# Opening reordered in a two-block LoRA kernel: one index table, the first weight split between tile pieces, GpSimd's subtractions behind a wait

## The reference

```python
# block 0: dense product and a mixture of 8 low-rank experts (rank 16), two chosen per token
base = einsum('btd,od->bto', x, W)
logits = einsum('btd,ed->bte', x, Wr) + 5.0 * one_hot(language_ids)
topw, topi = top_k(logits, 2)
gates = sum(one_hot(topi) * softmax(topw)[..., None], axis=-2)
h = einsum('btd,erd->bter', x, A)
x = x + base + 2.0 * einsum('bter,bte,eor->bto', h, gates, B)
# block 1: each batch has one of 64 adapters of rank 16, picked by adapter_ids
Bx = einsum('bni,bri->bnr', x, B1[adapter_ids])
x = x + einsum('bnr,bor->bno', Bx, A1[adapter_ids])
```

## Time and profile before

| what | value |
|---|---|
| median of the runs | 99.25 us |
| the profiled execution, its own time | 99.71 us |
| its span, first to last instruction | 97.4 us |
| TensorE (PE) busy | 92.1 us, 95% |
| VectorE busy | 62.2 us, 64% |
| ScalarE busy | 43.7 us, 45% |
| GpSimd busy | 37.4 us, 38% |
| mean granted TensorE clock | 1.00 |
| DMA | 14.36 MB, 147 GB/s |

### The profile page before, as it was taken

How to read it: one execution, slowest core, us unless ns; L and a number is a source line. 1 busy time by engine, 2 the same in 40 slices (tenths; PEclk the granted TensorE clock), 3 DMA queues, 4 the chain that set the end, 5 groups by cost and what they waited for, 6 DMA issues and landing times.

```text
span 97.4 us, 2162 instructions
## 1 busy us (share of the span) xinstructions
PE 92.1 (95%) x733; PEld 77.5 (80%) x733; DVE 62.2 (64%) x215; ACT 43.7 (45%) x88; POOL 37.4 (38%) x44
## 2 busy tenths in 40 slices
PE   4997899999999999999999999999999999999960
PEld 1596788889978788888978898889978897898950
DVE  4163999822297939891089749890199569881980
ACT  2552559240699991089207990099019700000300
POOL 5000778998920049995000069990000370000000
PEclk9999999999999999999999999999999999999999
DMA  1999947438983594235522922227000003241066
GB/s 20 353 279 340 429 156 224 97 73 271 382 202 83 124 367 93 51 71 159 153 60 47 344 98 108 108 50 274 5 0 0 3 7 127 88 172 43 7 211 220
DMA packets 14987, 14.36 MB, mean 147 GB/s; under 512 B 10112, under 2 KB 11392, under 8 KB 14592
## 3 DMA queue, kind: packets, MB, share of 16 engines
q1 hardware_dynamic: 14048, 11.85, 37.9%
q0 software_dynamic: 640, 2.10, 6.9%
q10 hardware_dynamic: 288, 0.28, 1.1%
HBM read 10.02 MB, written 4.19 MB: 146 GB/s over the span
## 4 chain that ended last, share of the span: by engine, by line
PE 84%; DMA 6%; DVE 4%; SPq 1%; ACT 1%; issue 0%; DVEq 0%
PE main L635 16%; PE main L641 15%; PE main L647 15%; PE aw_ps L677 11%; DMA xs<-x_t 6%; PE side L729 6%; PE main L662 4%; PE main L661 4%; PE main L663 4%; PE aw_ps L753 3%; DVE xs L530 2%; PE side L709 2%; PE main L753 1%; PE side L753 1%; SPq L212 1%; DVE x_lo L441 1%
## 5 line engine op out<-in xcount | busy, mean ns | idle before, releaser
L318 POOL TENSOR_TENSOR x_lo<-xs,x_hi 128x512 fp32r<-128x512 f32 x12 | 16.1, 1379 | 19.9 <-ACT x_hi L338 19.9
L635 PE MATMUL main<-x_hi,w_hi 128*128 128x512 f32 (+1 forms) x64 | 17.7, 398 | 0.5 <-DVE w_hi L565 0.5
L641 PE MATMUL main<-x_hi,w_lo 128*128 128x512 f32 (+1 forms) x64 | 16.9, 385 | 0.0
L647 PE MATMUL main<-x_lo,w_hi 128*128 128x512 f32 (+1 forms) x64 | 16.8, 384 | 0.0
L677 PE MATMUL aw_ps<-aws,xs 128*128 128x136 f32 x112 | 14.6, 284 | 0.0
L677 PEld LDWEIGHTS aw_ps<-aws,xs 128*128 128x128 f32 x112 | 14.2, 195 | 0.2
L370 ACT ACTIVATE a_ops<-a_hi 64x512 fp32r<-64x512 f32 x12 | 7.6, 630 | 14.5 <-POOL a_rest L292 14.3
L641 PEld LDWEIGHTS main<-x_hi,w_lo 128*128 128x128 f32 x64 | 11.8, 188 | 2.6
L647 PEld LDWEIGHTS main<-x_lo,w_hi 128*128 128x128 f32 x64 | 11.8, 188 | 2.4
L635 PEld LDWEIGHTS main<-x_hi,w_hi 128*128 128x128 f32 x64 | 11.3, 188 | 2.9 <-DVE w_hi L565 0.7
L489 DVE TENSOR_TENSOR xs<-main,xs 128x512 f32<-128x512 f32 x15 | 9.9, 683 | 2.1 <-PE main L663 2.1
(11 more groups left out here) (107 smaller groups left out, 136.2 us busy)
## 6 DMA issues: line engine op xcount, KB each, us to landing
out_t<-xs SPq DMA_DIRECT2D x16, 256.0 KB, 2.2
xs<-x_t SPq DMA_DIRECT2D x3, 1024.0 KB, 5.3
b1s<-b_t SPq DMA_DIRECT2D x64, 32.0 KB, 2.1
xs<-x_t SPq DMA_DIRECT2D x4, 256.0 KB, 4.1
ws<-w_t SPq DMA_DIRECT2D x4, 256.0 KB, 6.3
b0s<-b_t SPq DMA_DIRECT2D x1, 256.0 KB, 6.5
aws<-aw_t ACTq DMA_DIRECT2D x1, 204.0 KB, 3.9
rows<-a_t,row_at POOLq DMA_INDIRECT x8, 3.6
```

Source lines behind the costliest of these rows:

```text
L318: nc.gpsimd.tensor_tensor(x_lo[:, t % 2, c], xs[:, t, c], x_hi[:, t % 2, c].bitcast(F32), ALU.subtract).then_inc(x_lo_ready, 1)
L635: nc.tensor.matmul(out_ap, w_hi[:, c, k], x_hi[:, s, k, n], start=(k == 0), stop=False)
L641: nc.tensor.matmul(out_ap, w_lo[:, c, k], x_hi[:, s, k, n], start=False, stop=False)
L647: last = nc.tensor.matmul(out_ap, w_hi[:, c, k], x_lo[:, s, k, n], start=False, stop=False)
```

## The change

Four things change. The two index tables become one array and one DMA, issued behind weight block 1 where they were issued behind block 0. On VectorE the two halves of weight block 0 come after two of the four `x_lo` pieces and not after all four. The rest part of weight block 3 is done before the gates of tile 0, not after them. On GpSimd the first `x_lo` subtraction of tile 1 waits also for `b0_lo_ready`, which VectorE's `b_lo` gives.

```diff
@@ SyncE
             sp.dma_start(ws[:, 0], w[:, 0]).then_inc(w_loaded[0], 16)
-            sp.dma_start(language_ids[:], language_id.rearrange("p (t j) -> p t j", t=NB)).then_inc(language_loaded, 16)
-            sp.dma_start(adapter_ids[:], adapter).then_inc(adapter_loaded, 16)
             sp.dma_start(ws[:, 1], w[:, 1]).then_inc(w_loaded[1], 16)
+            sp.dma_start(ids[:], id_table).then_inc(ids_loaded, 16)
             sp.dma_start(ws[:, 2], w[:, 2]).then_inc(w_loaded[2], 16)
@@ GpSimd
-            pool.wait_ge(adapter_loaded, 16)
+            pool.wait_ge(ids_loaded, 16)
...
                     for c in range(K):
                         pool.wait_ge(x_hi_ready, t * K + c + 1)
+                        if t == 1 and c == 0:
+
+                            pool.wait_ge(b0_lo_ready, 1)
                         if t >= 2 and c == 0:
                             pool.wait_ge(base_done, (t - 1) * K)
@@ VectorE
-            for c in range(K):
+            def x0_rest(c):
                 dve.wait_ge(x_hi_ready, c + 1)
                 split_lo(x_lo[:, 0, c], xs[:, 0, c], x_hi[:, 0, c], x0_lo_ready)
+
+            x0_rest(0)
+            x0_rest(1)
             dve.wait_ge(w_loaded[0], 16)
             nc.vector.tensor_copy(w_hi[:, 0], ws[:, 0]).then_inc(w0_hi_ready, 1)
             dve.wait_ge(w0_hi_ready, 1)
             split_lo(w_lo[:, 0], ws[:, 0], w_hi[:, 0], w0_lo_ready)
-
-            dve.wait_ge(language_loaded, 16)
+            x0_rest(2)
+            x0_rest(3)
+
+            dve.wait_ge(ids_loaded, 16)
...
             w_rest(2)
+            w_rest(3)
             gate_h(0)
-            w_rest(3)
             dve.wait_ge(b0_hi_ready, 1)
             split_lo(b0_lo[:], b0s[:], b0_hi[:], b0_lo_ready)
```

More of the change, by code:

```diff
@@ L51, with two_block_kernel @@
 WARM = 6
-def two_block_kernel(nc, x, adapter, language_id, w, aw, b0, a1, b1, out, *, tokens_per_batch,
+def two_block_kernel(nc, x, id_table, w, aw, b0, a1, b1, out, *, tokens_per_batch,
                      experts, rank, adapters):
@@ L131, in two_block_kernel @@
         IDS = NG + NG * BPG
-        adapter_ids = sb("adapter_ids", [P, IDS], I32)
+        ids = sb("ids", [P, IDS + NB * TILES], I32)
+        adapter_ids, language_ids = ids[:, 0:IDS], ids[:, IDS:]
         wrap = sb("wrap", [P, IDS], I32)
@@ L137, in two_block_kernel @@
         row_at = sb("row_at", [P, NG], I32)
-        language_ids = sb("language_ids", [P, NB, TILES], I32)
         is_language = sb("is_language", [P, NB, TILES, experts])
@@ L143, in two_block_kernel @@
         side = [psum(f"side{i}") for i in range(2)]
-        adapter_loaded, language_loaded = sem("adapter_loaded"), sem("language_loaded")
+        ids_loaded = sem("ids_loaded")
         x0_loaded = [sem(f"x0_loaded{c}") for c in range(K)]
@@ L292, in split_a1 @@
                 nc.gpsimd.tensor_tensor(lo, rows[:, s], hi.bitcast(F32), ALU.subtract).then_inc(a1_lo_ready, 1)
-            pool.wait_ge(adapter_loaded, 16)
-            nc.gpsimd.tensor_scalar(wrap[:], adapter_ids[:], 0.0, float(adapters), ALU.is_lt,
+            pool.wait_ge(ids_loaded, 16)
+            nc.gpsimd.tensor_scalar(wrap[:], adapter_ids, 0.0, float(adapters), ALU.is_lt,
                                     ALU.mult).then_inc(index_step, 1)
             pool.wait_ge(index_step, 1)
-            nc.gpsimd.tensor_tensor(wrapped[:], wrap[:], adapter_ids[:], ALU.add).then_inc(index_step, 1)
+            nc.gpsimd.tensor_tensor(wrapped[:], wrap[:], adapter_ids, ALU.add).then_inc(index_step, 1)
             pool.wait_ge(index_step, 2)
@@ L567, in _ @@
             split_lo(w_lo[:, 0], ws[:, 0], w_hi[:, 0], w0_lo_ready)
-            dve.wait_ge(language_loaded, 16)
+            x0_rest(2)
+            x0_rest(3)
+            dve.wait_ge(ids_loaded, 16)
             then_wait(nc.vector.tensor_tensor(
                 is_language[:].rearrange("p t j e -> p (t j) e"),
-                language_ids[:].rearrange("p t j -> p (t j)").unsqueeze(2).broadcast_to([P, NB * TILES, experts]),
+                language_ids.unsqueeze(2).broadcast_to([P, NB * TILES, experts]),
                 expert_no[:].unsqueeze(1).broadcast_to([P, NB * TILES, experts]), ALU.is_equal))
@@ L839 @@
         "x_t": x.reshape(NB, TB, K, P).transpose(3, 0, 2, 1),
-        "adapter": np.concatenate([np.repeat(adapter.reshape(-1, P // R).T, R, axis=0),
-                                   np.broadcast_to(adapter.reshape(1, B), (P, B))], axis=1),
-        "language_id": np.repeat(language.reshape(-1, P // T).T, T, axis=0),
+        "id_table": np.concatenate([np.repeat(adapter.reshape(-1, P // R).T, R, axis=0),
+                                    np.broadcast_to(adapter.reshape(1, B), (P, B)),
+                                    np.repeat(language.reshape(-1, P // T).T, T, axis=0)], axis=1),
         "w_t": w.reshape(K, P, K, P).transpose(3, 0, 2, 1),
```

## The result

Before 99.25 us, after 100.7 us (four runs each, 99.03 to 99.54 before and 100.36 to 100.86 after); ratio 1.0145, 95% interval [1.0118, 1.0172]. The profiled execution of the changed kernel took 100.74 us with a span of 99.0 us. (Ratios leave out executions well above a kernel's fastest; where a kernel's executions spread widely, all are given.)

The account below looks back on a forecast made before the run. TensorE, busy 95%, was the bound, fed by a slackless chain from GpSimd's first `x_lo`. GpSimd's four subtractions would end at 23.87 instead of 21.45 us: 99.25 + 2.42 = 101.7 us, range 101.0 to 102.8 us.

Parts of the forecast that it names:

- The chain: GpSimd's first `x_lo`, gathers, `a_rest`, eight copies, exponential, gates, tile 1 transposes, TensorE: no slack, so all shift by 2.42 us.
- So I take 5.08 us: Length of GpSimd's four tile 1 subtractions in their new place, against 5.96 us beside VectorE's `w_lo` and `b_lo`.
- Gain at the front: 0.02 us, at most 0.05: Earlier cast of weight block 0 on VectorE gains little, since the weight lands only at 9.50 us.
- it ends at 18.70 us: End of VectorE's `b_lo`, started at 18.01 us and taking 0.69 us; GpSimd's subtractions start behind it at 18.79 us.
- the term of 2.42 us: Shift of all behind GpSimd's four subtractions, which end at 23.87 us instead of 21.45 us.
- the cast of block 0 comes much earlier: Sign of being wrong: VectorE's cast comes much earlier than about 9.5 us and TensorE starts before 9.9 us.
- R4: Rival, chance 0.05: VectorE reaches `b_lo` 0.5 us earlier, or TensorE has slack before tile 1's transposes; shift 1.8 us, 101.0 us.
- It is hidden in every place I can find: The index table's later landing delays neither language mask, gathers, `a_hi` nor `b1` rows enough to cost time.
- The 0.5 us that I took for it: Assumed delay of the index table behind weight block 1, between 0 and 1.3 us.
- front gains: Any small gain at TensorE's start is swallowed by its later wait before the second transposes.
- over 2 us: TensorE's expected wait for the gated `h` before the second set of transposes, with L635 behind it near 35.4 us.
- R2: Rival, chance 0.06: TensorE's clock falls after idling 2.4 us at 32.4 us, losing 1.4 us more; 103.1 us.

## Why the prediction was right in kind and wrong in size

- The chain was right: the hold delays `a_rest`, this the copies and the exponential, and TensorE waits at the second transposes. The changed trace shows each link, the hold alone costs 0.6 us, and moving the exponential out of the chain won 0.6 to 0.7 us in both kernels.
- "So I take 5.08 us": right, 5.02 us in all four profiles with the hold on `b_lo`.
- "Gain at the front: 0.02 us, at most 0.05", and with it "it ends at 18.70 us": this is the step that failed. I took the landing of one profiled execution as the kernel's. Block 0 landed 1.0 us earlier in the changed profile, and 0.5 to 1.6 us earlier in the others; the cast came at 8.48 us, and `b_lo` ended at 17.43 us, 1.27 us before its forecast. Of these, 1.04 us are the cast; in the other 0.23 us VectorE's list behind the cast was shorter than I had reckoned. GpSimd's run ended at 22.60 us instead of 23.87, so the term of 2.42 us measured 22.60 - 21.45 = 1.15 us. The whole change cost 1.03 us between the profiled executions and 1.45 us between the medians. That "the cast of block 0 comes much earlier" was among my own signs of being wrong. R4 had named the place, `b_lo` reached earlier, but by 0.5 us and for other reasons.
- Why the same opening matters less in the kernel before: there GpSimd's run waits only for `x_hi` of tile 1, and its start moved by 0.4 to 0.5 us (15.01 us with an early opening, in the kernel with the early exponential, against 15.39 and 15.49 us in the two profiles of before). Under the hold GpSimd hangs on VectorE's whole list from block 0 on. This would make the gap between the medians larger than that between the profiles, as it is; but no profile of the kernel before itself caught an early opening, so it is argued and not shown.
- "It is hidden in every place I can find", of the index table: wrong outside the hold. Alone it makes 99.2 to 102.6 us of 99.2. The clash is shown for the profiled execution, at 100.41 us; for the slower ones it is likely and not shown. In the changed kernel the hold hides it: GpSimd's gathers ended 1.6 us before its run began. The 0.5 us that I took for it can't be read from the profiles: GpSimd's index arithmetic began at 9.90 and 9.32 us in the kernel before, and at 10.60 and 9.55 us in the changed one.
- The 1 us that TensorE gained at the front was lost again, as the prediction said of front gains. TensorE reached `down_part` 1.02 us earlier than before (27.06 against 28.08 us), began `base(1, 0)` 0.47 us later (29.82 against 29.35), and the L642 behind the second transposes 1.18 us later (33.90 against 32.72). So it lost 1.5 us at `down_part`, of which one wait of 0.68 us is marked, and 0.7 us at the transposes, 0.53 marked. The prediction named only the second place; the first came from `gap` beside `a_rest`, which it did not see. The "over 2 us" of waiting before the transposes did not come.
- R2: no clock fall in the changed kernel. Its longest wait behind TensorE's start was 0.68 us in one profile and 0.99 us in the other, and the grant stayed at 1.00. The mechanism did show elsewhere: with waits of 4.09 and 2.75 us the grant fell to 0.50, with one of 1.72 us (the table alone) it stayed at 1.00. No run had the wait of 2.4 us that R2 was about.
- The question that the prediction did not ask is what the hold replaces. Without it the new order takes 105.3 us. The clash was in the earlier trace rows (1.26 and 1.77 us), and I used it only to price GpSimd's run and `b_lo`.

## What to carry to other kernels

A wait on a second engine may be there to keep two engines' SBUF instructions apart: before pricing it, look which short instructions would fall into the other's run, and what stands behind them. Where the shared work can move to an engine that idles there, no wait is needed. And a landing time from one execution is a sample: ask what your sum does if every load comes 1 us earlier.

## What the runs showed of the hardware

- VectorE instructions of 0.16 to 0.69 us took up to 5.41 us beside GpSimd's subtractions. `denom` (a tensor_scalar, one SBUF input; 5.34 us) and `gap` (two SBUF inputs; 1.80 us) ended within 0.03 us of GpSimd's run; `w_lo` (two; 5.41 us) ended 0.56 us behind it, where it takes 0.69 us alone. `recip` (0.18 us), the gated products and the x1 additions (a PSUM input) kept their time.
- The Trainium skill, "SBUF — State Buffer", section "SBUF: two separate sides", calls the port pair that the two engines share "an exclusive lock, not a bandwidth split". By it, a VectorE instruction in a 2-port mode, or one with two SBUF inputs beside a GpSimd instruction that reads SBUF, shuts the other engine out or is shut out, and the one that starts first holds the pair for its whole instruction. The traces agree for those with two SBUF inputs; in which mode `denom` ran, no view shows. They show more: the wait can last over four of GpSimd's instructions back to back (5.34 and 5.32 us for `denom`, 5.41 for `w_lo`), or over one (1.27 us). What decides between these was not found. In the three profiles with the long wait, GpSimd's run followed its gather at once; in the four where VectorE got in between, GpSimd had waited 0.3 to 1.0 us before it began.
- Loads issued within 0.04 us of the same time landed 6.5 to 8.2 us from the span's start (fourth x piece) and 7.9 to 9.5 us from it (weight block 0).
